# Reordering the first preparation of a gated mixture layer, and holding back two of its weight loads

## The chip, the cores and the metric

The kernel runs on one core of one Trainium2 chip. The metric is device time in microseconds (us) for one execution of the whole program, as the median of several runs. The profile is one further execution. Its view is given from the start of its span, and an engine is named as in the profile: PE is the tensor engine's matmul side, PEld its weight loads, DVE the vector engine, ACT the scalar engine, POOL GpSimd, SP the sync engine, whose work here is only to issue DMAs. ACTq and SPq are DMA issues by ACT and SP.

## The reference, cut to what matters

Four batches of 512 tokens with 512 channels pass one decoder layer in three stages, each closed by a residual and a LayerNorm:

```
x = layernorm(x + linear_attention(x))             # gated, 16 heads
x = layernorm(x + experts(x, fside, ctx))          # per batch an int8-style pair of linears
x = layernorm(x + gated_ffn(x))                    # top-2 of 8 LoRA experts

# experts, first linear (_smooth_quant_linear), per batch, w = fside[batch]:
amax_x = max|x| over tokens, amax_w = max|w| over rows     # the channel maxima
s  = sqrt(amax_x / amax_w); xs = x / s; ws = w * s         # then both are quantised by row

# gated_ffn:
logits = x @ gate_w.T;  top_w, top_i = top_k(logits, 2);  routing = softmax(top_w)
h1 = x @ w1.T + 2 * x @ A1.T @ B1.T    (h3 alike; A and B are the chosen expert's)
act = silu(h1) * h3;  out += routing * (act @ w2.T + 2 * act @ A2.T @ B2.T)
```

The precision is kept by splitting each fp32 operand into a high and a low part (`_hi`, `_lo`) and making three matmuls of each product (`matmul_split`, lines 116 to 118).

## The kernel before, in words

The program has two halves. The first half (up to 421 us in the profile) computes attention for all four batches with the quantised experts of batch 0 folded into it. The second half, the function `mixture`, runs over the four batches. For batch b it computes the gated layer of b and, threaded between its matmuls, the quantised experts of batch b+1. Every engine has its own program in it, and semaphores order them.

`mixture` has three kinds of section on each engine. `prepare(0)` runs once, ahead of everything. `hidden(b, ...)` runs over the 11 tiles f of the inner dimension: PE makes `f_h` (h1 in bank h1, h3 in bank h3) from the transposed tokens `f_xT` and the up-weights `f_up`, ACT takes silu, DVE weighs and multiplies. `between(b, ...)` makes the down matmuls and, beside them, the preparation for b+1. This case is about `prepare(0)`, for which there are no matmuls of another tile to run beside it.

What `prepare(0)` has to deliver:

- SP reloads x1 of batch 1 from DRAM into `tokens` (`load_expert_tokens`, line 1449) and fills the three slots of `f_up` with up tiles 0, 1 and 2 (`load_up`, line 1441). Then it goes on to `hidden`, where its first wait is for the end of tile 0.
- ACT issues the load of `fside[1]` into `weights` (`load_weights(0, 0)`, line 1617). That memory held the raw adapters before.
- PE makes the transposes of x, the logits by token (`logits_across`, `logits_by_token` L2250, in bank LT), and the adapters' inner products U1 and U3 in banks `f_z_sum` and `f_z_second`. Then it waits for DVE: `masks_transposed` (L2270) for the masks, `weights_spread` (L2280) for the routing weights, `first_maxima` (L2292) for the channel maxima and for `um_ready` at 4.
- DVE computes, from the logits, the choice of experts (`choose`, lines 1816 to 1840: 21 small instructions), the softmax weights (`weigh`, 1846 to 1850, with an exponential on ACT between), the masked adapters (`mask_adapters`, L1862, four products into `f_work`) and their low parts (`adapters_lo`, L1868). It also computes the channel maxima over token rows: `channel_top(b, 0, 0)` from `tokens` and `channel_top(b, 0, 1)` from `weights`, both L1931, both into `f_q_mem`. The second waits for the DMA of `weights`.
- ACT turns the masked adapters into high parts (`masked_hi`, L1589) and then writes `f_weightT` (`weights_out`, L1585). PE's first `f_h` matmul waits for the latter.

Engines take their instructions strictly in the order written. `first_maxima` reuses banks `f_z_sum` and `f_z_second`, and so comes after the masked adapters:

```
def first_maxima(b):
    for i, item in enumerate((MX0, MW0)):
        pe.wait_ge(top_ready, PRIMED + 4 * b + i + 1)
        if i == 0:
            pe.wait_ge(um_ready, PRIMED + 4 * b + 4)
```

Of the kernel before, what the change touches and what calls it, by code (L numbers as in the profile page):

```python
# [41 lines left out]
PRIMED = 1  # L42
# [1188 lines left out]
SLOTS = 3  # L1231
# [15 lines left out]
def mixture(nc, shared, used, x1_dram, x2_dram, up_dram, w1, w2, down_stream, descending, out_dram):  # L1247
# [9 lines left out]
    with ExitStack() as ctx:  # L1257
# [5 lines left out]
        def sem(name):  # L1263
            primed.append(ctx.enter_context(nc.semaphore("f_" + name)))
            return primed[-1]
# [108 lines left out]
        we_loaded = sem("we_loaded")  # L1374
# [26 lines left out]
        def slot(b, item):  # L1401

            k = BANK[item]
            return k, b * len(BANK_ORDER[k]) + BANK_ORDER[k].index(item)
# [5 lines left out]
        def place(b, key):  # L1410

            n = EXPERT_ORDER.index(key)
            return n % RING, b * EXPERT_PER_BANK + n // RING

        def batches(eng, prepare, hidden, between):


            prepare(0)
            with eng.Fori(0, B - 2) as b:
                hidden(b, True)  # L1420
                between(b, True, True)
            hidden(B - 2, True)
            between(B - 2, True, False)
            hidden(B - 1, False)
            between(B - 1, False, False)

        def tiles(b, f):
            return b * FT + f + 1
# [4 lines left out]
        @block.sync  # L1433
        def _(sp):
            sp.dma_start(desc[:, :], descending).then_inc(consts_loaded, 16)
            sp.dma_start(x2_dram[0:T, :].rearrange("(t p) d -> p t d", p=P), x2[:, :, :]).then_inc(x2_stored, 16)

            SLOT_USES = [len(range(r, FT, SLOTS)) for r in range(SLOTS)]

            def load_up(f):  # L1440
                sp.dma_start(up[:, f % SLOTS, :, :].bitcast(F32), up_dram[f, :, :, :])\
                    .then_inc(up_loaded[f % SLOTS], 16)

            def load_x3(source):
                sp.dma_start(x3[:, :, :], source.rearrange("(t p) d -> p t d", p=P)).then_inc(x3_loaded, 16)

            def load_expert_tokens(b):

                sp.dma_start(xe[:, :, :], x1_dram[bass.ts(b, T), :].rearrange("(t p) d -> p t d", p=P))\
                    .then_inc(xe_loaded, 16)  # L1450

            def tokens_transposed(b):
                for c in (KT - 1, KT - 2):
                    k, before = slot(b, XC0 + c)
                    sp.wait_ge(filled[k], PRIMED + before + 1)

            def store(b):
                for h in range(2):
                    sp.wait_ge(normed, PRIMED + b * TT + 2 * h + 2)
                    sp.dma_start(out_dram[bass.ds(b * T + h * 2 * P, 2 * P), :].rearrange("(t p) d -> p t d", p=P),  # L1460
                                 x3[:, 2 * h:2 * h + 2, :]).then_inc(out_stored, 16)

            def prepare(b):
                tokens_transposed(0)
                sp.wait_ge(x2_stored, PRIMED + 16)
                load_expert_tokens(0)
                for f in range(SLOTS):
                    load_up(f)

            def hidden(b, expert):  # L1470
                for f in range(FT - SLOTS):
                    sp.wait_ge(z_done, PRIMED + tiles(b, f))
                    load_up(f + SLOTS)
                    if f == 0:
                        sp.wait_ge(out_stored, PRIMED + 32 * b)
                        if expert:
                            load_x3(x1_dram[bass.ts(b, T), :])
                        else:
                            sp.wait_ge(x2_stored, PRIMED + 16 * (b + 1))
                            load_x3(x2_dram[bass.ts(b, T), :])  # L1480

            def between(b, expert, another):
                if expert:
                    sp.wait_ge(z_done, PRIMED + tiles(b, FT - 2))
                    load_up(0)
                    sp.wait_ge(summed, PRIMED + TT * (b + 1))
                    load_x3(x2_dram[bass.ts(b, T), :])
                    tokens_transposed(b + 1)
                    if another:
                        sp.wait_ge(x2_stored, PRIMED + 16 * (b + 2))  # L1490
                        load_expert_tokens(b + 1)
                    load_up(1)
                    load_up(2)
                store(b)

            batches(sp, prepare, hidden, between)
            sp.wait_ge(out_stored, PRIMED + 32 * B)

# [293 lines left out]
        def _(dve):  # L1792
# [12 lines left out]
            def x_lo(b, c):  # L1805
                k, n = slot(b, XC0 + c)
                dve.wait_ge(xT_hi_ready, PRIMED + b * KT + c + 1)
                dve.tensor_tensor(xT_lo[:, c, :], bank[k][:, :], xT_hi[:, c, :].bitcast(F32), ALU.subtract)\
                    .then_inc(drained[k], 1)
# [33 lines left out]
            def weigh(b):  # L1843

                dve.wait_ge(exp_ready, PRIMED + b + 1)
                dve.tensor_scalar(soft[:, 2, :], soft[:, 1, :], 1.0, None, ALU.add).then_inc(weight_ready, 1)
                dve.wait_ge(weight_ready, PRIMED + 3 * b + 1)
                dve.reciprocal(weight[:, 0, :], soft[:, 2, :]).then_inc(weight_ready, 1)
                dve.wait_ge(weight_ready, PRIMED + 3 * b + 2)
                dve.tensor_tensor(weight[:, 1, :], soft[:, 1, :], weight[:, 0, :], ALU.mult).then_inc(weight_ready, 1)  # L1850

            def mask_adapters(b):

                k, n = slot(b, MT)
                dve.wait_ge(drained[k], PRIMED + n + 1)
                for item in (U1, U3):
                    k, n = slot(b, item)
                    dve.wait_ge(filled[k], PRIMED + n + 1)
                for a in range(2):
                    for i, item in enumerate((U1, U3)):  # L1860
                        k, n = slot(b, item)
                        ins = dve.tensor_tensor(um[:, 2 * a + i, :], bank[k][:, :], maskT[:, a, :], ALU.mult)  # L1862
                        ins.then_inc(um_ready, 1)

            def adapters_lo(b):
                for a in range(4):
                    dve.wait_ge(um_hi_ready, PRIMED + 4 * b + a + 1)
                    dve.tensor_tensor(umT_lo[:, a, :], um[:, a, :], umT_hi[:, a, :].bitcast(F32), ALU.subtract)\  # L1868
                        .then_inc(um_lo_ready, 1)

            def prepare(b):
                x_lo(b, 0)
                x_lo(b, 1)
                dve.wait_ge(consts_ready, PRIMED + 3)
                dve.tensor_tensor(a_lo[:, :, :], a_raw, a_hi[:, :, :].bitcast(F32), ALU.subtract)\
                    .then_inc(consts_ready, 1)
                dve.tensor_tensor(b2_lo[:, :], b2_raw, b2_hi[:, :].bitcast(F32), ALU.subtract)\
                    .then_inc(consts_ready, 1)
                x_lo(b, 2)
                x_lo(b, 3)  # L1880
                for i in range(2):
                    channel_top(b, 0, i)
                dve.wait_ge(consts_loaded, PRIMED + 16)
                choose(b)
                weigh(b)
                mask_adapters(b)
                adapters_lo(b)
                channel_ratio(b, 0)
                channel_scale(b, 0)
# [29 lines left out]
            def channel_top(b, which, i):  # L1919

                C = CHANNELS[which]
                if i:
                    dve.wait_ge(we_loaded, PRIMED + 32 * b + 16 * which + 16)
                    if which:
                        k, n = place(b, (0, XT1))
                        dve.wait_ge(e_filled[k], PRIMED + n + 1)
                elif which == 0:
                    dve.wait_ge(xe_loaded, PRIMED + 16 * b + 16)
                else:
                    dve.wait_ge(e_act_ready, PRIMED + b + 1)  # L1930
                dve.tensor_reduce(top[:, i, 0:C], (xe, we)[i][:, :, 0:C].rearrange("p t c -> p c t"),  # L1931
                                  AX.X, ALU.max, apply_absolute_value=True).then_inc(top_ready, 1)
# [182 lines left out]
            def between(b, expert, another):  # L2115
# [14 lines left out]
                normalise(b, expert, another)  # L2130

            batches(dve, prepare, hidden, between)

        @block.tensor
# [406 lines left out]
```

## Time and profile before

| | us |
|---|---|
| median of 3 runs (lowest, highest) | 1150.32 (1149.33, 1150.97) |
| profiled execution, its own time | 1150.53 |
| its span | 1148.7 |
| PE busy | 1042.4 (91%) |
| DVE busy | 708.4 (62%) |
| ACT busy | 403.9 (35%) |
| POOL busy | 288.5 (25%) |

The profiled execution's time is 1.8 us more than its span (what lies around the first and the last instruction), and 0.2 us above the median. The granted clock of TensorE is 1.0 where it runs at 2.4 GHz and 0.50 at 1.2 GHz. Its mean over the span is 0.954. The busy shares are means over stages with different limits. What is asked here is what one stage of some 47 us costs, from 421 us, where the first half ends, to 468 us, where the first `f_h` matmul starts.

### The profile page before, as it was taken

Reading aid. Unit: us, or ns where it says so; the run is one execution under the profiler, and the core shown is the slowest. Engines: PE = TensorE matmul, PEld = TensorE weight load, DVE = VectorE, ACT = ScalarE, POOL = GpSimd, SP = SyncE. Lnnn points to the kernel's source line nnn. Section 1 sums busy time; section 2 is a strip of 40 time slices with the busy share of each in tenths; the row PEclk is TensorE's granted clock in tenths of the full one; section 3 lists DMA queues with packets and bytes.
Section 4 is the critical chain, followed back from the end, with each engine's and each line's share of the span. In section 5 each row is a group of like instructions: output and inputs, shape, how many; then the busy total and the mean of one; then the engine's idle time right before and its main releaser. Section 6 shows DMA issues by size and latency. Waiting matters only on the chain.

```text
span 1148.7 us, 14072 instructions
## 1 busy us (share of the span) xinstructions
PE 1042.4 (91%) x4920; PEld 820.0 (71%) x4920; DVE 708.4 (62%) x1150; ACT 403.9 (35%) x623; POOL 288.5 (25%) x239
## 2 busy tenths in 40 slices
PE   4899999999589635899999999999999999999997
PEld 3677777777477523777777777877777777878885
DVE  6544745746686744766764976773985864555542
ACT  4232423423134321453424253533343434322221
POOL 3245455554342110200142110131120132100021
PEclk9899999999899666899999999999999999999999
DMA  7013342532410016052446144337133417044421
GB/s 266 26 60 120 132 158 88 192 135 88 166 28 1 29 40 258 1 206 101 164 165 221 39 156 148 114 137 284 55 137 120 160 69 279 28 165 151 164 69 56
DMA packets 47852, 142.88 MB, mean 124 GB/s; under 512 B 3496, under 2 KB 14632, under 8 KB 42160
## 3 DMA queue, kind: packets, MB, share of 16 engines
q1 hardware_dynamic: 28720, 118.71, 28.2%
q10 hardware_dynamic: 19072, 23.35, 6.3%
q8 instruction: 39, 0.64, 0.2%
q14 instruction: 21, 0.17, 0.0%
HBM read 114.66 MB, written 27.39 MB: 124 GB/s over the span
## 4 chain that ended last, share of the span: by engine, by line
PE 41%; DVE 12%; DMA 3%; issue 3%; ACT 2%; POOL 1%; DVEq 0%; ACTq 0%
PE f_h L116 7%; PE f_h L118 7%; PE f_h L117 7%; PE f_h L2170 3%; PE f_y L116 3%; PE f_y L118 3%; PE f_y L117 3%; DMA f_down_raw<-in_down_stream 2%; DMA weights<-in_w 2%; DVE f_work L1911 2%; DVE f_work L1903 2%; PE f_y L2360 1%; DVE f_row_max L1981 1%; DVE f_q_mem L1931 1%; PE f_z_sum L116 1%
## 5 line engine op out<-in xcount | busy, mean ns | idle before, releaser
L116 PE MATMUL f_h<-f_xT_hi,f_up 128*128 128x512 f32 x352 | 139.8, 397 | 1.8 <-issue 1.1
L117 PE MATMUL f_h<-f_xT_hi,f_up 128*128 128x512 f32 x352 | 137.9, 392 | 0.0
L118 PE MATMUL f_h<-f_xT_lo,f_up 128*128 128x512 f32 x352 | 137.2, 390 | 0.0
L116 PE MATMUL ring<-w_hi,xT_hi 128*128 128x512 f32 x256 | 111.2, 434 | 15.1 <-DVE w_lo L754 15.1
L1503 POOL TENSOR_TENSOR f_down_lo<-f_down_raw,f_down_hi 128x512 fp32r<-128x512 f32 x44 | 61.0, 1389 | 229.6 <-ACT f_down_hi L1553 229.6
L1708 ACT ACTIVATE f_work<-f_h 128x512 f32<-128x512 f32 x88 | 52.4, 595 | 169.8 <-PE f_h L2170 114.5
L1903 DVE TENSOR_TENSOR f_work<-f_work,f_weightT 128x512 f32<-128x512 f32 x88 | 65.4, 743 | 70.0 <-ACT f_work L1708 69.0
L1514 POOL TENSOR_TENSOR weights<-weights,f_rows 128x512 f32<-128x512 f32 (+1 forms) x24 | 33.3, 1418 | 292.1 <-ACT f_rows L1635 182.5
L1911 DVE TENSOR_TENSOR f_work<-f_h,f_work 128x512 f32<-128x512 f32 x88 | 60.9, 692 | 70.1 <-PE f_h L118 64.8
L118 PE MATMUL ring<-w_lo,xT_hi 128*128 128x512 f32 x256 | 104.0, 406 | 0.0
L117 PE MATMUL ring<-w_hi,xT_lo 128*128 128x512 f32 x256 | 103.9, 406 | 0.0
L116 PEld LDWEIGHTS f_h<-f_xT_hi,f_up 128*128 128x128 f32 x352 | 66.1, 188 | 17.1 <-issue 2.3
L118 PEld LDWEIGHTS f_h<-f_xT_lo,f_up 128*128 128x128 f32 x352 | 66.1, 188 | 14.7
L117 PEld LDWEIGHTS f_h<-f_xT_hi,f_up 128*128 128x128 f32 x352 | 66.2, 188 | 14.0
L475 POOL TENSOR_TENSOR rot_b<-qk,ropes 128x256 f32<-128x256 f32 x64 | 55.5, 888 | 81.7 <-ACT qk L575 81.7
L116 PEld LDWEIGHTS ring<-w_hi,xT_hi 128*128 128x128 f32 x256 | 50.0, 195 | 32.0 <-issue 17.2
L116 PE MATMUL f_y<-f_down_hi,f_both_hi 128*128 128x512 f32 x176 | 72.5, 412 | 0.0
L117 PE MATMUL f_y<-f_down_hi,f_both_lo 128*128 128x512 f32 x176 | 71.1, 404 | 0.0
L118 PE MATMUL f_y<-f_down_lo,f_both_hi 128*128 128x512 f32 x176 | 70.8, 402 | 0.0
L2170 PE MATMUL f_h<-f_umT_hi,f_up 128*128 128x512 f32 x176 | 57.7, 409 | 11.4 <-DVE f_work L1911 11.4
L1602 ACT ACTIVATE f_second_hi<-f_work 128x512 fp32r<-128x512 f32 x44 | 27.9, 635 | 107.9 <-DVE f_work L1911 107.9
L575 ACT ACTIVATE qk<-ring 128x512 f32<-128x512 f32 x32 | 19.1, 597 | 121.0 <-PE ring L1063 121.0
(305 smaller groups left out, 2276.5 us busy)
## 6 DMA issues: line engine op xcount, KB each, us to landing
f_up<-up_scratch SPq DMA_DIRECT2D x44, 1408.0 KB, 6.1
f_down_raw<-in_down_stream ACTq DMA_DIRECT2D x44, 256.0 KB, 3.5
weights<-in_up_stream SPq DMA_DIRECT2D x11, 704.0 KB, 5.1
up_scratch<-tokens SPq DMA_DIRECT2D x11, 704.0 KB, 3.1
up_scratch<-scaled_w SPq DMA_DIRECT2D x11, 704.0 KB, 3.5
f_x<-x_scratch SPq DMA_DIRECT2D x7, 1024.0 KB, 8.6
x_tok<-in_x SPq DMA_DIRECT2D x4, 1024.0 KB, 5.5
out<-f_x SPq DMA_DIRECT2D x8, 512.0 KB, 3.0
```

The lines of the kernel that those rows point to most:

```text
L116: pe.matmul(out, lhs_hi, rhs_hi, start=start, stop=False)
L117: pe.matmul(out, lhs_lo, rhs_hi, start=False, stop=False)
L118: return pe.matmul(out, lhs_hi, rhs_lo, start=False, stop=stop)
L475: pool.tensor_tensor(b4[:, :, :, two], q4[:, :, :, 1 - two], sin[:, :, two].unsqueeze(1).to_broadcast([P, H, DK // 2]), ALU.mult).then_inc ...
L575: act.activation(qk[:, bass.ts((PQ, PK).index(item), D)], ring[k][:, :], ACT.Copy)\
L1503: pool.tensor_tensor(down_lo[:, f % DOWNS, :], down_raw[:, f % DOWNS, :], down_hi[:, f % DOWNS, :].bitcast(F32), ALU.subtract).then_inc(do ...
L1514: pool.tensor_tensor(we[:, t, 0:C], we[:, t, 0:C], rows[:, 1, 0:C], ALU.mult).then_inc(w_scaled, 1)
L1602: sc.activation(second_hi[:, :], act[:, 1, :], ACT.Copy).then_inc(act_hi_ready, 1)
L1708: sc.activation(silu[:, choice, :], h_ps[0][:, :], ACT.Silu).then_inc(silu_ready, 1)
L1903: dve.tensor_tensor(silu[:, choice, :], silu[:, choice, :], weightT[:, choice, :], ALU.mult)\
L1911: dve.tensor_tensor(act[:, choice, :], h_ps[1][:, :], silu[:, choice, :], ALU.mult)\
L2170: last = pe.matmul(h_ps[i][:, :], weights(f, l, cols), r[:, rhs, :], start=False, stop=True, skip_group_check=True)
```

## The change

Two edits, both in `prepare(0)` alone. On DVE, the choice of experts and their weights are put between the two channel maxima: the maxima of `tokens` stay in front, those of `weights` come behind `weigh` and ahead of `mask_adapters`. On SP, only up tile 0 is loaded at once. SP then waits until the DMA of `weights` has landed, and issues up tiles 1 and 2 after that. Instructions, shapes and data are the same, except for that one wait on SP.

```
@@ prepare(0) on SP
                 tokens_transposed(0)
                 sp.wait_ge(x2_stored, PRIMED + 16)
                 load_expert_tokens(0)
-                for f in range(SLOTS):
+                load_up(0)
+                sp.wait_ge(we_loaded, PRIMED + 16)
+                for f in range(1, SLOTS):
                     load_up(f)
@@ prepare(b) on DVE
                 x_lo(b, 2)
                 x_lo(b, 3)
-                for i in range(2):
-                    channel_top(b, 0, i)
+                channel_top(b, 0, 0)
                 dve.wait_ge(consts_loaded, PRIMED + 16)
                 choose(b)
                 weigh(b)
+                channel_top(b, 0, 1)
                 mask_adapters(b)
                 adapters_lo(b)
                 channel_ratio(b, 0)
```

## Rows read from the trace of the kernel before

**Rows 1.** Who waited for whom, 425 to 475 us: total, times, longest.

```profile
PE f_h L2270 <- DVE f_work L1840: 12.7, 1, 12.7
DVE f_q_mem L1931 <- DMA weights<-in_w: 10.3, 1, 10.3
```

**Rows 2.** Chain that ended last, 430 to 476 us: start us, us, what.

```profile
435.25 18.60 DMA weights<-in_w
...
461.64 1.05 PE f_h L2270 x8
...
463.77 0.70 DVE f_work L1862
464.49 2.42 ACT f_umT_hi L1589 x4
466.92 0.98 ACT f_weightT L1585 x2
...
468.14 0.49 PE f_h L116
468.63 0.23 PE f_h L117
```

**Rows 3.** DVE in order of time, 439 to 463 us: start us, us, instruction.

```profile
439.77 3.76 DVE L1931 TENSOR_REDUCE f_q_mem<-tokens 128x512 f32<-128x2048 f32 x1 [3.36 <-DMA tokens<-x_scratch]
453.87 3.62 DVE L1931 TENSOR_REDUCE f_q_mem<-weights 128x512 f32<-128x2048 f32 x1 [10.34 <-DMA weights<-in_w]
457.41 0.18 DVE L1816 COPY f_logits<-f_h 128x32 f32<-128x32 f32 x1
...
461.91 0.16 DVE L1850 TENSOR_TENSOR f_weight<-f_soft,f_weight 128x4 f32<-128x4 f32 x1
```

**Rows 4.** PE in order of time, 441 to 467 us: start us, us, instruction.

```profile
441.22 0.63 PE L118 MATMUL f_h<-f_xT_lo,f_a_hi 128*8 128x512 f32 x1
441.64 0.63 PE L116 MATMUL f_z_sum<-f_xT_hi,f_a_hi 128*128 128x512 f32 x1
...
444.90 1.05 PE L2250 MATMUL f_h<-ident,f_work 8*128 8x8 f32 x8
...
448.53 0.40 PE L118 MATMUL f_z_second<-f_xT_lo,f_a_hi 128*128 128x512 f32 x1
...
462.47 3.73 PE L2280 MATMUL f_h<-ident,f_weight 128*128 128x128 f32 x16
466.40 0.63 PE L2292 MATMUL f_z_sum<-ident,f_q_mem 128*128 128x128 f32 x4 [0.20 <-DVE f_work L1862]
```

**Rows 5.** DMA issues, 434 to 440 us: count, KB each, median us to landing.

```profile
f_up<-up_scratch SPq DMA_DIRECT2D x3, 1408.0 KB, 14.2
tokens<-x_scratch SPq DMA_DIRECT2D x1, 1024.0 KB, 5.7
```

**Rows 6.** DMA queues from 440 to 450 us (q1 is SP's, q10 ACT's): packets, MB, share.

```profile
q1 hardware_dynamic: 341, 3.48, 83.0%
q10 hardware_dynamic: 344, 0.70, 18.4%
```

**Rows 7.** Line 1617, the load of `weights`, over all six of its issues.

```profile
DMA to landing us min/median/max: 3.9/5.3/18.6
```

**Rows 8.** Line 2280 in the next batch, 596 to 792 us: busy us, mean ns.

```profile
L2280 PE MATMUL f_h<-ident,f_weight 128*128 128x128 f32 x16 | 1.9, 275 | 0.0
```

**Rows 9.** Windows: length, busy us (count) of PE, PEld, DVE, ACT, POOL, granted clock, DMA, GB/s.

```profile
343.60:347.00 3.40, 3.21 (x16) 2.93 (x17) 3.30 (x5) 3.38 (x6) 0.00 (x0) 0.52 0.00 0
...
412.50:415.30 2.80, 0.00 (x0) 0.00 (x0) 2.77 (x5) 0.00 (x0) 2.80 (x3) 0.97 0.00 0
...
436.50:442.60 6.10, 6.04 (x15) 2.51 (x16) 2.83 (x1) 0.70 (x2) 0.00 (x0) 0.51 1.04 424
...
448.90:452.80 3.90, 0.02 (x1) 0.00 (x0) 0.00 (x0) 0.00 (x0) 0.00 (x0) 0.99 0.67 273
...
461.60:466.50 4.90, 4.66 (x25) 4.40 (x26) 3.13 (x8) 3.03 (x5) 0.00 (x0) 0.52 0.00 2
```

More of the change, by code:

```diff
@@ L1466, in prepare @@
                 load_expert_tokens(0)
-                for f in range(SLOTS):
+                load_up(0)
+                sp.wait_ge(we_loaded, PRIMED + 16)
+                for f in range(1, SLOTS):
                     load_up(f)
@@ L1880, in prepare @@
                 x_lo(b, 3)
-                for i in range(2):
-                    channel_top(b, 0, i)
+                channel_top(b, 0, 0)
                 dve.wait_ge(consts_loaded, PRIMED + 16)
@@ L1885, in prepare @@
                 weigh(b)
+                channel_top(b, 0, 1)
                 mask_adapters(b)
```

## The prediction, made before the changed kernel had run

> **What bounds the kernel now.** I read four views in this order. The page says that PE is busy for 91% of the span, so a gain has to come from a place where PE stands idle. The waits around the start of `mixture` name such a place: PE stood 12.7 us in one piece ahead of L2270, the transposes of the masks, waiting for `choose`; and in the same stretch DVE stood 10.3 us ahead of L1931 for the DMA of `weights` [rows 1]. The chain says that both waits are one: it runs from the load of `weights`, issued at 435.25 and 18.60 us long, through DVE, to the masks on PE at 461.64, the masked adapters at 463.77, ACT's high parts and `f_weightT`, to the first `f_h` matmul at 468.14 [rows 2]. The timelines then show that the wait is due to order and not to need. The logits by token, all that `choose` reads, are complete when L2250 ends, at 444.90 + 1.05 = 445.95 [rows 4]. DVE has finished the maxima of `tokens` at 439.77 + 3.76 = 443.53 and then stands in front of a reduction of `weights` until 453.87; `choose` starts behind it at 457.41 [rows 3]. PE has had nothing to do since its last U3 matmul, 448.53 + 0.40 = 448.93 [rows 4].
>
> All that follows in the program hangs on that first `f_h` matmul: `hidden`, `between` and the later batches go from semaphore to semaphore, with no anchor in absolute time. A shift of its start should reach the end whole.
>
> **The change, part by part.**
>
> *When `choose` and `weigh` run.* They take from 457.41 to 461.91 + 0.16 = 462.07, so 4.66 us, ACT's exponential included [rows 3]. In the new order DVE is free at 443.53 and waits for the logits at 445.95. With a hand-off of about 0.05 us, `weigh` is complete at 445.95 + 0.05 + 4.66 = 450.66. ACT has nothing else to do there, so the exponential is as prompt as now.
>
> *The maxima of `weights`.* This reduction of 3.62 us [rows 3] now stands between `weigh` and `mask_adapters`. If the data are there by 450.66, it ends at 454.28, or 454.25 with the small overlap of successive DVE instructions that rows 3 show (453.87 + 3.62 is 457.49, the next starts at 457.41). Behind it on DVE are `mask_adapters`, `adapters_lo` and `channel_ratio`, and behind those all of `hidden`, so a late `weights` would still hold up everything.
>
> *When `weights` land.* Between 440 and 450 us both queues were full. SP's queue moved 3.48 MB in 341 packets and ACT's 0.70 MB in 344 [rows 6]. So `weights`, with small packets, got a sixth of the bandwidth while the three up tiles (1408 KB each [rows 5]) were under way. `tokens`, issued first, landed after 5.7 us, about 439.8, and this doesn't change [rows 5]. With one up tile in place of three, 1.44 MB at SP's rate of 0.348 MB/us is 4.1 us, so up tile 0 is done by about 443.5. `weights` then has 0.3 of its 1.05 MB. The other 0.75 MB at the summed rate of 0.42 MB/us is 1.8 us; with one or two us for the last packets, it lands between 445 and 447. The bounds: the fastest landing of this load is 3.9 us [rows 7], but not ahead of `tokens`, so about 440, and the slowest is as now, 453.85. Anything before 450.66 is worth the same. I take 446, as these are byte counts of the same transfers, which leaves 4 to 5 us of slack.
>
> *The held-back up tiles.* SP's wait ends at 446, and both tiles then take 2.88 MB at 0.42 MB/us, 7 us, with 2 us of latency: landed by about 455. Even if SP were released only at 453.9, it would be 463. PE wants up tile 1 only for f = 1, after the 30 matmuls and more of f = 0, some 10 us behind the first `f_h` matmul (in the old trace 478.7, so about 470 in the new). The edit costs nothing, and what hides it is tile 0. If the cover were gone the price would be the lateness itself. What is queued behind the waiting instruction on SP are these two loads, then a wait for the end of tile 0 that comes long after. Nobody else waits for SP.
>
> *From the masked adapters to PE.* The masks on PE start at about 450.3, and `f_maskT` is there two us later (1.05 and 1.03 us on PE and ACT now), before DVE is free at 454.25. So `mask_adapters` starts at 454.25 in place of 463.77 [rows 2]: 9.5 us earlier. From it to the first `f_h` matmul now takes 468.14 - 463.77 = 4.37 us over ACT's 2.42 and 0.98 us [rows 2], of which nothing changes: 458.6 in place of 468.1.
>
> *TensorE's clock.* This is the term that I can't read off. Now the clock fell some 3.9 us after PE stopped at 448.9, and in another place 2.8 us after PE stopped at 412.5 [rows 9]. PE then ran at half clock from 461.6 to 466.5, and the clock was back when the first `f_h` matmul came [rows 9]. In the new order PE stops for 1.4 us, transposes the masks, and spreads the weights in 1.9 us at full clock [rows 8] in place of 3.73 at half [rows 4], so until about 452.7. It then waits for all four masked adapters, 454.25 + 2.6 = 456.85 (they end so long after their start: 466.40 against 463.77 [rows 2, 4]). That is an idle gap of 4.1 us, as long as those behind which it fell. So I take it that the clock is at half when `first_maxima` starts. Eight transposes at half clock take about 2.0 us (16 took 3.73), ending at 458.85, so the first `f_h` matmul is at 458.85 and not 458.6: 0.25 us lost. After a restart the clock was back after 3.4 us in the quickest case, 4.9 us in the stage in question, and 6.1 us in the slowest of these [rows 9]. From 456.85 that is 460.3, 461.8 or 463.0, so `f_h` runs at half clock for 1.4 to 4.2 us. An `f_h` matmul starts 0.23 us after the one before it at full clock [rows 2] and one of that size 0.42 at half [rows 4], so 45% of that stretch is lost: 0.6 to 1.9 us. PE's first 30 matmuls of f = 0 are on the chain without a gap, so nothing hides this. I take 1.6 us, toward the long end, as the restart is interrupted by short gaps. Below nothing is not possible here, since the `f_h` matmuls already run at full clock.
>
> The Trainium skill, "TensorE: Matmul & The Clock Gate", section "Why this matters for your kernels", speaks against this change in part: it advises against idle stretches between matmul bursts, since the clock goes back to half behind them, and the new order leaves one right in front of the long run of `f_h`. By that rule the term is paid and the time is 1142.6; without it, 1140.8. The trace bears the rule out in both falls [rows 9], and no row shows a gap of that length that kept the clock.
>
> **The sum.** 9.5 - 0.25 - 1.6 = 7.7 us less. Against the profiled execution's 1150.53 that is 1142.8 (its span 1148.7 would become 1141.0). The median of the runs is 0.2 lower, so 1142.6.
>
> **The rivals.**
>
> *The clock doesn't fall, or the half-clock stretch is hidden.* The gain is the whole 9.5 us: 1140.8. For it: a little PE work, the masks and weights, now lies inside what was one long pause. Against: the gap of 4.1 us that stays behind it, and 2.8 us that were enough in rows 9.
>
> *`weights` still land late* (the two held-back tiles weren't what slowed it, so that half of the change does nothing). Then DVE stands again until 453.9, the masked adapters start at 457.5, 6.3 us earlier than now, and with the clock's 1.8 us the gain is 4.5: 1145.8. For it: only that the last packets of this load came 1.5 us or more after the queues thinned out. Against: rows 6, by which it got a sixth of the bandwidth, and rows 7, by which the same load lands in 3.9 to 5.3 us where it isn't crowded.
>
> *The gain is lost again later.* If something in `hidden` of batch 0 were bound by a transfer or an engine that doesn't shift, the time would be 1150. I find none: x3, up tile 3 and `scale_weights` on POOL are all issued from the ends of tiles and shift with them.
>
> *Slower.* The one mechanism that I see is the clock: if it stays at half through the first tiles of `hidden`, each us there costs 0.45. It decides from 9.5 / 0.45 = 21 us on, so until about 480; at 27 us it costs 12 and the time is 1153. No row with PE fully busy shows more than 6.2 us at half.
>
> **How the numbers follow.** Forecast (a gain of 5.8 to 8.6, as the clock term is 0.9 to 3.7): 0.72. Clock hidden, 1140.8: 0.13. `weights` late, 1145.8: 0.09. Gain lost later: 0.03. Slower: 0.03. The range from 1140.0 to 1145.4 takes in both bounds of the clock term, the case without it and the spread of single runs (1149.3 to 1151.0 before), and leaves out about 0.15 or 0.2. A difference of 0.2% (2.3 us) is about what a measurement of this kernel can tell from no change. Faster by more than that: 0.94; within it: 0.03; slower: 0.03.
>
> **What the new profile would show.** DVE's wait for `weights` gone, or under 0.5 us, with that load landing some 10 to 12 us after its issue in place of 18.6. L1816 right behind L2250, at about 446. L1931 on `weights` at about 450.7. L1862 at about 454.3. PE's wait ahead of L2270 down from 12.7 to 1.4 us, and a new one of about 4 us ahead of L2292 on L1862. The first `f_h` matmul at about 458.8, several of them at half clock, and the clock back between 460 and 463. No wait for up tile 1. From tile 1 on the same intervals as now, 7 to 8 us earlier. The prediction is wrong if `weights` land after 450.7, if the clock behaves otherwise, or if a later stage starts to wait for something new.

## The result and the profile after

The changed kernel takes 1141.76 us (median of 4 runs, 1140.74 to 1143.54) against 1150.53 before (4 runs, 1149.33 to 1150.97). The ratio is 0.9927, with a 95% interval of 0.991 to 0.9944, so it is 0.7% faster. The profiled execution has a span of 1140.4 us and a mean granted clock of 0.961, against 1148.7 and 0.954.

These are the waits of the changed kernel from 425 to 475 us (total, times, longest). Its lines lie two further down than before (L2270 is L2272 now).

```profile
PE f_z_sum L2294 <- DVE f_work L1864: 3.6, 1, 3.6
DVE f_q_mem L1933 <- DMA tokens<-x_scratch: 3.2, 1, 3.2
...
DVE f_logits L1818 <- PE f_h L2252: 2.6, 1, 2.6
...
PE f_h L2272 <- DVE f_work L1842: 1.4, 1, 1.4
```

Both waits of [rows 1] have turned into what was foreseen. DVE no longer waits for `weights` at all. PE waits 1.4 us for the masks in place of 12.7, and a new wait of 3.6 us stands ahead of `first_maxima`. The timeline of DVE shows the order and the times:

```profile
428.33 0.06 DVE L1795 MEMSET f_round_bias<- 128x1 f32 x1 [8.31 <-PEq L145]
...
438.70 3.77 DVE L1933 TENSOR_REDUCE f_q_mem<-tokens 128x512 f32<-128x2048 f32 x1 [3.24 <-DMA tokens<-x_scratch]
445.11 0.19 DVE L1818 COPY f_logits<-f_h 128x32 f32<-128x32 f32 x1 [2.64 <-PE f_h L2252]
...
449.70 3.65 DVE L1933 TENSOR_REDUCE f_q_mem<-weights 128x512 f32<-128x2048 f32 x1
453.27 0.68 DVE L1864 TENSOR_TENSOR f_work<-f_z_sum,f_maskT 128x512 f32<-128x512 f32 x1
```

The memset at 428.33 is DVE's first instruction in `mixture`. In the trace of before it stands at 429.29:

```profile
429.29 0.06 DVE L1793 MEMSET f_round_bias<- 128x1 f32 x1 [8.32 <-PEq L145]
```

So `mixture` starts 0.96 us earlier in this execution, after a first half that the change doesn't touch. It is chance: in the other traces of this document the memset stands anywhere from 426.67 to 429.79, and in the changed kernel's second one at 429.73. All comparisons of stages below are therefore made from that memset. The masked adapters start 24.94 us behind it (453.27 - 428.33) and not 34.48 us (463.77 in [rows 2], less 429.29): 9.54 us less. PE and its clock:

```profile
449.84 2.41 PE L2282 MATMUL f_h<-ident,f_weight 128*128 128x128 f32 x16
455.89 1.08 PE L2294 MATMUL f_z_sum<-ident,f_q_mem 128*128 128x128 f32 x4 [3.64 <-DVE f_work L1864]
456.76 1.06 PE L2294 MATMUL f_z_second<-ident,f_q_mem 128*128 128x128 f32 x4
457.63 0.79 PE L116 MATMUL f_h<-f_xT_hi,f_up 128*128 128x512 f32 x1
458.22 0.63 PE L117 MATMUL f_h<-f_xT_hi,f_up 128*128 128x512 f32 x1
458.64 0.63 PE L118 MATMUL f_h<-f_xT_lo,f_up 128*128 128x512 f32 x1
...
466.65 0.63 PE L2172 MATMUL f_h<-f_umT_hi,f_up 128*128 128x512 f32 x2
```

The same stretch in windows (length, busy us of PE, PEld, DVE, ACT and POOL with counts, granted clock, DMA share, GB/s):

```profile
452.30:455.40 3.10, 0.00 (x0) 0.00 (x0) 3.10 (x5) 1.42 (x3) 0.00 (x0) 0.96 0.65 272
455.50:462.10 6.60, 6.21 (x19) 5.10 (x20) 4.79 (x12) 3.36 (x6) 0.00 (x0) 0.51 0.00 0
462.30:466.60 4.30, 4.30 (x20) 3.54 (x19) 0.69 (x1) 1.88 (x2) 0.00 (x0) 1.00 0.00 0
```

The clock fell at about 455.2, 2.9 us after PE had stopped at 452.25, and came back at about 462.0, so 4.4 us of `f_h` ran at half. The reader sees it in the matmuls as well: they start 0.43 us apart at 458.22 and 458.64, where [rows 2] have 0.23. The 30 matmuls of f = 0 ahead of L2172 take 466.65 - 457.63 = 9.02 us. In the trace of before they took 475.12 - 468.14 = 6.98:

```profile
475.12 0.63 PE L2170 MATMUL f_h<-f_umT_hi,f_up 128*128 128x512 f32 x2
```

So the half clock cost 2.04 us. The transfers of the changed kernel between 434 and 475 us (count, KB each, median us to landing):

```profile
f_up<-up_scratch SPq DMA_DIRECT2D x3, 1408.0 KB, 9.3
weights<-in_w ACTq DMA_DIRECT2D x1, 1024.0 KB, 11.7
```

`weights` was issued at 434.29 and landed at 446.0, 11.7 us after its issue in place of 18.6.

### The profile page after: what moved, and what is told of

The parts are those of the page before. It is cut to its first block, busy times and chain, and to the rows that moved or that the text cites. A ratio compares the mean times of both kernels' runs of the same rounds, so it can differ in the third digit from the quotient of the medians.

```text
span 1140.4 us, 14072 instructions
## 1 busy us (share of the span) xinstructions
PE 1038.0 (91%) x4920; PEld 816.6 (72%) x4920; DVE 708.3 (62%) x1150; ACT 404.0 (35%) x623; POOL 289.1 (25%) x239
## 4 chain that ended last, share of the span: by engine, by line
PE 41%; DVE 14%; issue 3%; ACT 2%; DMA 2%; DVEq 0%; ACTq 0%
PE f_h L116 7%; PE f_h L117 7%; PE f_h L118 7%; PE f_h L2172 4%; PE f_y L116 2%; PE f_y L118 2%; PE f_y L117 2%; DMA f_down_raw<-in_down_stream 2%; DVE f_work L1913 2%; DVE f_q_mem L1933 2%; DVE f_work L1905 2%; PE f_y L2362 1%; PE f_z_sum L116 1%; PE f_z_sum L117 1%; DVE f_row_max L1983 1%
## 5 line engine op out<-in xcount | busy, mean ns | idle before, releaser
L116 PE MATMUL f_h<-f_xT_hi,f_up 128*128 128x512 f32 x352 | 140.8, 400 | 0.6 <-issue 0.6
L116 PE MATMUL ring<-w_hi,xT_hi 128*128 128x512 f32 x256 | 111.1, 434 | 15.1 <-DVE w_lo L754 15.1
L116 PEld LDWEIGHTS f_h<-f_xT_hi,f_up 128*128 128x128 f32 x352 | 66.6, 189 | 16.0 <-issue 1.1
L116 PEld LDWEIGHTS ring<-w_hi,xT_hi 128*128 128x128 f32 x256 | 50.0, 195 | 32.0 <-issue 17.2
L116 PE MATMUL f_y<-f_down_hi,f_both_hi 128*128 128x512 f32 x176 | 70.6, 401 | 0.0
L2172 PE MATMUL f_h<-f_umT_hi,f_up 128*128 128x512 f32 x176 | 57.7, 409 | 12.2 <-DVE f_work L1913 12.2
```

The source lines that it names most:

```text
L116: pe.matmul(out, lhs_hi, rhs_hi, start=start, stop=False)
L2172: last = pe.matmul(h_ps[i][:, :], weights(f, l, cols), r[:, rhs, :], start=False, stop=True, skip_group_check=True)
```

## The experiments

Two measures are given for each run. One is the median over 4 to 6 runs, which moves by about one us between groups of runs (the changed kernel gave 1141.76 and, a second time, 1142.76; the kernel before gave 1150.53, 1149.98 and 1150.34). The ratio is taken to the runs of the kernel before that stood beside each group. The other, from the profile, is the stage: from the memset that opens `mixture` on DVE to the first L2172 (L2170), the end of the first 30 `f_h` matmuls. It is split where `f_h` starts. Each of its parts repeats within 0.05 us in the two profiles of the changed kernel, so it separates what the medians can't.

| kernel | to first `f_h` | 30 `f_h` matmuls | stage | median | ratio to before, 95% |
|---|---|---|---|---|---|
| before | 38.85 | 6.98 | 45.83 | 1150.53 | |
| changed | 29.30 | 9.02 | 38.32 | 1141.76 | 0.9927 (0.991 to 0.9944) |
| changed, again | 29.33 | 9.02 | 38.35 | 1142.76 | 0.9935 (0.9916 to 0.9954) |
| loads held, old order | 32.00 | 6.98 | 38.98 | 1144.98 | 0.9961 (0.9945 to 0.9976) |
| new order, loads not held | 32.46 | 7.57 | 40.03 | 1146.74 | 0.9964 (0.995 to 0.9978) |
| changed, clock kept | 29.35 | 7.00 | 36.35 | 1140.54 | 0.9918 (0.9904 to 0.9931) |
| only tile 2 held | 29.27 | 8.99 | 38.26 | 1143.13 | 0.9941 (0.9924 to 0.9957) |
| all three held | 29.32 | 9.02 | 38.34 | 1142.44 | 0.9933 (0.9913 to 0.9954) |
| all held, split maxima | 27.51 | 9.80 | 37.31 | 1142.15 | 0.9929 (0.9913 to 0.9945) |
| the same, clock kept | 27.58 | 6.99 | 34.57 | 1138.65 | 0.9895 (0.9878 to 0.9913) |

**Each half of the change alone.** The edit on SP without the one on DVE:

```
-                for f in range(SLOTS):
+                load_up(0)
+                sp.wait_ge(we_loaded, PRIMED + 16)
+                for f in range(1, SLOTS):
                     load_up(f)
```

> The kernel before with the edit on SP alone: up tiles 1 and 2 wait for weights, DVE keeps its old order. My theory, from the traces of before and after: weights land about 446, as in the changed kernel, so DVE stands some 3.5 us for them in place of 10.3, choose runs behind the second maxima from about 449.6 and the masked adapters start at about 455.9 (7 us earlier than before, 2.6 us later than in the changed kernel). PE's restart from the masks to the first f_h matmul is then one nearly unbroken run, as before the change, so the clock should be back to 2.4 GHz when f_h starts and nothing is paid for it: 7 us faster than before, 1143.6, and only some 1 to 2 us slower than the changed kernel although its masked adapters are 2.6 us later. First rival, that the order of DVE's work is what helped and the loads don't matter: no change, 1150.5. Second rival, that the clock costs the same here: 1145.5.

And the edit on DVE without the one on SP:

```
-                for i in range(2):
-                    channel_top(b, 0, i)
+                channel_top(b, 0, 0)
                 dve.wait_ge(consts_loaded, PRIMED + 16)
                 choose(b)
                 weigh(b)
+                channel_top(b, 0, 1)
                 mask_adapters(b)
```

> The changed kernel with all three up tiles loaded at once again: the edit on DVE alone. My theory: weights land 18.6 us after their issue, at about 452.9, the second maxima end at 456.5 and the masked adapters start there, 6.3 us earlier than before; PE stands from about 452 to 459, so the first f_h matmuls run at half clock and some 1.9 us is lost: 4.4 us faster than before, 1146.1. First rival, that the two loads didn't slow weights: the same as the changed kernel, 1141.8. Second rival, no cost of the clock: 1144.2.

With the loads held and the old order, DVE and PE did this:

```profile
446.11 3.73 DVE L1933 TENSOR_REDUCE f_q_mem<-weights 128x512 f32<-128x2048 f32 x1 [3.70 <-DMA weights<-in_w]
...
456.13 0.69 DVE L1864 TENSOR_TENSOR f_work<-f_z_sum,f_maskT 128x512 f32<-128x512 f32 x1 [1.70 <-ACT f_maskT L1580]
...
460.55 0.49 PE L116 MATMUL f_h<-f_xT_hi,f_up 128*128 128x512 f32 x1 [0.72 <-ACT f_weightT L1587]
```

and in windows

```profile
452.00:458.70 6.70, 4.56 (x24) 4.26 (x24) 4.76 (x16) 3.08 (x6) 0.00 (x0) 0.50 0.37 156
458.90:467.50 8.60, 7.88 (x38) 6.42 (x38) 4.96 (x12) 4.72 (x7) 0.00 (x0) 1.00 0.00 0
```

The masked adapters start 27.6 us after the memset (at 428.55 here), 6.9 us less than before, and the clock is back at about 458.7, before `f_h` begins; PE had been at work since 454.0. The stage is 6.85 us shorter, as the theory had it, and the rival that only the order matters falls. The median is only 5.0 us below that of the kernel before in the runs beside it (1149.98), 1144.98 where 1143.6 was expected. In its profile 0.7 us of the stage's gain are lost after the stage, and that profile is of the fastest of the six executions (1143.57). The rest is not explained.

With the new order and the loads not held, DVE waited for `weights` again, and PE longer than in any other run with the new order:

```profile
454.21 3.62 DVE L1931 TENSOR_REDUCE f_q_mem<-weights 128x512 f32<-128x2048 f32 x1 [3.07 <-DMA weights<-in_w]
457.75 0.68 DVE L1862 TENSOR_TENSOR f_work<-f_z_sum,f_maskT 128x512 f32<-128x512 f32 x1
...
460.37 1.09 PE L2292 MATMUL f_z_sum<-ident,f_q_mem 128*128 128x128 f32 x4 [6.77 <-DVE f_work L1862]
```

and, in the window from PE's restart until the clock was back,

```profile
460.40:463.40 3.00, 3.00 (x11) 2.61 (x12) 2.97 (x6) 2.74 (x4) 0.00 (x0) 0.51 0.00 0
```

`weights` took 18.6 us to land, exactly as before the change, so the two up tiles are what slowed it. The masked adapters start 6.4 us earlier than before (28.10 against 34.48), as expected (6.3). The clock was back 3.0 us after PE's restart at 460.37, when 1.25 us of `f_h` had passed, so it cost 0.6 us and not 1.9, and the stage is 5.8 us shorter where 4.4 was expected. The median of 1146.74 lies near the expected 1146.1 all the same, which is chance: in this profile 1.5 us of the stage's gain are lost again after the stage.

What follows: each half does most of the work alone, 6.85 and 5.8 us in the stage, and both together give 7.5 and not 12.7. They remove the same wait from two sides. What holding the loads adds to the new order is 3.2 us in the start of `f_h`, and what the order adds to the held loads is 2.7, of which the clock takes back 2.0.

**The clock.** The changed kernel with work for PE in its pause:

```
                 weights_spread(b)
+                for _ in range(14):
+                    pe.matmul(y_ps[0][:, :], a_hi[:, 0, 0:P], xT_hi[:, 0, :], start=True, stop=True)
                 first_maxima(b)
```

> The changed kernel with 14 further matmuls of 512 columns on PE between weights_spread and first_maxima, into a bank that nothing reads before it is overwritten. They fill the 3.6 us in which PE waits for the masked adapters. My theory: f_h starts at the same time, 457.6, but at full clock, so the 2.0 us that the half clock cost come back: 1139.7. Rival, that the half-clock stretch is hidden or that these matmuls run long and delay first_maxima: no change, 1141.8, or slower by what they overrun (14 x 0.23 = 3.2 us from 452.2 end at 455.5, before 455.9, so under 0.2 us at full clock, but 2.5 us if they ran at half clock).

```profile
452.40:456.10 3.70, 3.19 (x14) 2.30 (x14) 3.70 (x6) 1.89 (x4) 0.00 (x0) 1.00 0.59 249
456.10:464.80 8.70, 8.01 (x38) 6.58 (x39) 5.12 (x12) 4.87 (x7) 0.00 (x0) 1.00 0.00 0
```

The clock stayed at 2.4 GHz throughout. `f_h` starts at the same distance as in the changed kernel (29.35 and 29.30), and its 30 matmuls take 7.00 us in place of 9.02. So the half clock is the whole of those 2.0 us, and the rival, that they are hidden, falls. The median is 1140.54, 0.8 us above the expected 1139.7, and 1.2 to 2.2 us below the two medians of the changed kernel. The intervals of the ratios overlap, so it is the stage that shows the gain.

**How much slack the load of `weights` has.** With two up tiles at once in place of one:

```
                 load_up(0)
+                load_up(1)
                 sp.wait_ge(we_loaded, PRIMED + 16)
-                for f in range(1, SLOTS):
-                    load_up(f)
+                load_up(2)
```

> The changed kernel with up tiles 0 and 1 loaded at once and only tile 2 held back behind weights. By the byte counts (two tiles of 1.44 MB at 0.348 MB/us from about 438.3, then the rest of weights at 0.42 MB/us and one or two us for the last packets) weights land between 449 and 450.2, where DVE wants them at 449.7. My theory: a wait of DVE for weights of 0.5 us at the most, so the same time as the changed kernel, 1141.8, to 0.5 us more. Rival, that DVE reads weights while other loads slow it, or that tile 2 comes late for its use: a longer reduction than 3.65 us or a wait of PE for up tile 2, 1143 or more.

With none at once:

```
-                load_up(0)
                 sp.wait_ge(we_loaded, PRIMED + 16)
-                for f in range(1, SLOTS):
+                for f in range(SLOTS):
                     load_up(f)
```

> The changed kernel with all three up tiles held back behind weights and nothing else. My theory: weights land near 443, 3 us earlier than in the changed kernel, which nobody needs, since DVE gets to them at 449.7: the same stage time as the changed kernel, within 0.2 us, and 1141.8. Rival, that the changed kernel was still limited by the landing of weights: up to 2 us faster; or that up tile 0 is late: slower, with a wait of PE for f_up.

`weights` with two tiles beside it, and then with none:

```profile
weights<-in_w ACTq DMA_DIRECT2D x1, 1024.0 KB, 15.3
```

```profile
weights<-in_w ACTq DMA_DIRECT2D x1, 1024.0 KB, 7.5
```

So the landing takes 7.5, 11.7, 15.3 and 18.6 us with none, one, two and three tiles beside it (6.8 and 6.9 with none in the two runs with split maxima below): 3.3 to 4.2 us for each. At the rates of [rows 6], 1.44 MB take 3.4 us of both queues together and 4.1 of SP's alone. The stage is the same with none, one and two (38.34, 38.32, 38.26), and DVE has no wait for `weights` in any of them. With two it landed just in time, some 15.3 us after an issue about 6 us behind the memset, where DVE gets to it 21.3 us behind it. The expected wait of up to 0.5 us didn't appear, and neither did a late tile. To hold back one tile was enough for the profiled stage, by a margin too small to rely on. Its median of 1143.13 is 0.8 us above what was expected at the most, and the profile is of the fastest of the four executions (1140.47), so it can't be said that all of them were free of the wait. With all three held the median is 1142.44, and nothing is gained or lost in the stage, as expected.

**The order taken further.** All three tiles held, and the maxima of `weights` in two halves, the first in DVE's pause ahead of `choose`:

```
                 channel_top(b, 0, 0)
+                dve.wait_ge(we_loaded, PRIMED + 16)
+                weights_top(0)
                 dve.wait_ge(consts_loaded, PRIMED + 16)
                 choose(b)
                 weigh(b)
-                channel_top(b, 0, 1)
+                weights_top(1).then_inc(top_ready, 1)
                 mask_adapters(b)
...
+            def weights_top(half):
+                cols = bass.ts(half, D // 2)
+                return dve.tensor_reduce(top[:, 1, cols], we[:, :, cols].rearrange("p t c -> p c t"),
+                                         AX.X, ALU.max, apply_absolute_value=True)
```

> The changed kernel with all three up tiles held back behind weights, and the maxima of weights cut into two reductions of 256 columns each: the first in DVE's pause ahead of choose, the second where the whole stood, behind weigh. My theory: with no up tile beside it, weights land near 443, the first half runs to about 445 or 446, choose starts with or within 1 us of the logits (445.1), the second half ends near 452 and the masked adapters start there, 1.2 to 1.8 us earlier than in the changed kernel. PE's pause ahead of first_maxima shrinks from 3.6 to about 2 us. If the clock then stays up, the stage is 3.3 to 3.8 us shorter than in the changed kernel (1138.2); if it falls as it did, 1.2 to 1.8 us (1140.3). Rival, that up tile 0 comes too late for the first f_h matmul (issued at 443, it lands at about 449 by the same byte counts, 7 us ahead): a wait of PE for the DMA of f_up, and no gain, 1141.8.

```profile
448.80:453.00 4.20, 2.29 (x19) 1.91 (x16) 4.20 (x6) 2.84 (x5) 0.00 (x0) 1.00 0.75 318
453.10:454.30 1.20, 1.06 (x8) 0.82 (x8) 1.20 (x3) 1.20 (x3) 0.00 (x0) 0.91 0.00 0
454.50:461.10 6.60, 6.27 (x15) 4.95 (x16) 3.00 (x9) 1.57 (x3) 0.00 (x0) 0.52 0.00 0
```

`f_h` starts 1.8 us earlier than in the changed kernel (27.51 against 29.30), as expected, but its 30 matmuls take 9.80 us: the clock fell although the pause was only 1.9 us long, and stayed low for the first 6.1 us of `f_h`. Of the 1.8 us, 0.8 are lost so, and the median shows no difference from the changed kernel. Of the two forecasts the one with a falling clock was nearer, and even that was 0.2 to 0.8 us too good in the stage and 1.9 in the median. Up tile 0 was in time, so that rival falls. With PE kept busy in the pause as well:

```
                 weights_spread(b)
+                for _ in range(7):
+                    pe.matmul(y_ps[0][:, :], a_hi[:, 0, 0:P], xT_hi[:, 0, :], start=True, stop=True)
                 first_maxima(b)
```

> The kernel with the split maxima and all three up tiles held back, and with 7 further matmuls of 512 columns on PE between weights_spread and first_maxima, as in the run that kept the clock. My theory: both gains add, as the one is when the masked adapters start and the other is at what clock the first f_h matmuls run: f_h starts at about 456 at full clock, 10.9 to 11.3 us less in the stage than before, 1138.2. Rival, that the split alone keeps the clock: then this one is no faster than that, and slower by what the 7 matmuls overrun.

```profile
457.40:464.30 6.90, 6.90 (x30) 5.69 (x31) 3.29 (x9) 3.07 (x4) 0.00 (x0) 1.00 0.00 0
```

Both gains are there, 27.58 and 6.99 us, and the stage is 11.26 us shorter than before. The median of 1138.65 makes it the fastest of all; its interval (0.9878 to 0.9913) touches that of the changed kernel (0.991 to 0.9944) only at the edge.

The changed kernel once more, beside these:

> The changed kernel as it is, beside the others on the same chip. My theory: from the first instruction of mixture to the last h matmul of tile 0, 38.3 us in place of 45.8, of which the place where the clock rises can move 1 to 2 us from run to run; median 1141.8. Rival, none: this is the measure of the spread.

Its stage was 38.35 us, the same as the first time; the 1 to 2 us by which the rise of the clock was thought to move didn't appear. The profiled execution took 1145.41 us all the same, 3.2 more than the first one's 1142.24. Of these, 1.4 lie ahead of the memset and 1.8 behind the stage.

## Why the prediction was right

It forecast 1142.6, and the median is 1141.76 (1142.76 the second time). By its own steps:

- *When `choose` and `weigh` run.* Right. The logits' copy starts 0.11 us after L2252 ends (445.11 against 443.95 + 1.05 = 445.00), and the maxima of `weights` begin at 449.70, 4.6 us later.
- *The maxima of `weights`.* 3.65 us, in line with 3.62. That it lies on the path is shown by the split: 1.8 us of it taken off the path brought `f_h` forward by 1.8.
- *When `weights` land.* In the time of the old trace it landed at 446.0 + 0.96 = 447.0, at the late end of the 445 to 447 that I gave, and 1 us later than the 446 that I took. The working itself says 446.3 to 447.3 (443.5, 1.8, and one or two us). The slack was 3.7 us and not 4 to 5. The runs with none, two and three tiles beside it confirm the count of bytes.
- *The masked adapters.* 9.54 us earlier, 9.5 forecast.
- *The held-back tiles* cost nothing. The waits show none for `f_up`.
- *From the masked adapters to the first `f_h` matmul.* 4.36 us, with 4.37 before. The 0.25 us that I added for `first_maxima` at half clock isn't there. The `f_h` matmul waits for ACT's `f_weightT` too, and starts 0.26 us behind the end of it in both traces (457.63 and 457.37 after, 468.14 and 467.88 before); PE's slower transposes lie beside ACT's work. In all ten traces, at either clock, this stretch is 4.36 to 4.42 us. ACT before and after:

```profile
466.82 1.06 ACT L1585 ACTIVATE f_weightT<-f_h 128x512 f32<-128x512 f32 x2
```

```profile
456.31 1.06 ACT L1587 ACTIVATE f_weightT<-f_h 128x512 f32<-128x512 f32 x2
```

- *The clock.* That it falls, that it costs and that nothing hides the cost was right, and is shown by the run that kept the clock. The size was 2.04 us, where I had put 1.6 (1.85 with the 0.25) and 1.9 at the most: the clock was back 6.1 us after the restart, the slowest case of [rows 9], and 4.4 us of `f_h` ran at half. The 3.7 us that the chances use as the upper bound of this term follow from no row. The pause was 3.64 us and not 4.1, as the spread of the weights took 2.41 us at full clock and not the 1.9 of [rows 8]. The rule that the prediction weighed, from the Trainium skill, "TensorE: Matmul & The Clock Gate", section "Why this matters for your kernels", against idle stretches between bursts, holds here: the trace of the changed kernel agrees (the clock fell 2.9 us into a pause of 3.6), and to fill the stretch is worth what it cost.
- *The sum.* 7.7 us forecast, 7.51 us in the stage. The span fell by 8.3, which is these 7.5 and the 0.96 by which `mixture` began earlier, less 0.2 further on. That it came so close is luck in part: the 0.25 too much and the 0.44 too little work against each other, and the other kernels of this document paid anything from nothing to 2.8 us for the clock, which the old trace could not foretell.

That the stage's gain reaches the end whole was only argued. From the memset to the end of the span the program took 719.4 us before and 712.1 after, so in this pair of traces it is true but for 0.2 us. It isn't true of every trace: behind the stage the program takes 673.6 us before, 673.8 after and 673.7 to 673.8 in three of the experiments, but 675.5 in the changed kernel's second trace, 674.3 with the loads held alone and 675.1 with the order alone. In the second trace the cause is the clock. In the old trace it fell for a while near the end of `hidden` in batches 0 to 2, and in the first trace of the changed kernel it didn't. The same stretch, 585 to 600 us, in the old trace and in the new:

```profile
585.00:600.00 15.00, 12.60 (x48) 9.78 (x47) 10.43 (x21) 4.57 (x8) 4.86 (x4) 0.89 0.43 155
```

```profile
585.00:600.00 15.00, 12.71 (x60) 10.06 (x58) 6.01 (x11) 9.10 (x15) 4.25 (x4) 1.00 0.77 277
```

One would expect a further gain from the three dips that are gone. There is none, since PE waits there for ACT's normalised tokens: 13.19 us from the last L2170 of that `hidden` (L2172) to the transposes of the next batch in both traces, with 0.73 us of waiting in the old and 2.29 in the new.

```profile
591.76 0.40 PE L2170 MATMUL f_h<-f_umT_lo,f_up 128*128 128x512 f32 x1
604.95 1.06 PE L2231 MATMUL f_h<-ident,tokens 128*128 128x128 f32 x8 [0.73 <-ACT tokens L1677]
```

```profile
583.28 0.39 PE L2172 MATMUL f_h<-f_umT_lo,f_up 128*128 128x512 f32 x1
596.47 1.07 PE L2233 MATMUL f_h<-ident,tokens 128*128 128x128 f32 x8 [2.29 <-ACT tokens L1679]
```

The change didn't do away with the dips. The second trace of the same kernel has them again behind batches 1 and 2, and so has every trace of the experiments behind at least one batch. Where such a dip comes late it does cost time. This is the stretch around the transposes behind batch 2, in the first and in the second trace of the changed kernel:

```profile
950.57:960.57 10.00, 8.51 (x44) 5.75 (x45) 3.86 (x5) 5.17 (x9) 2.59 (x2) 1.00 0.76 249
```

```profile
952.00:962.00 10.00, 8.11 (x36) 6.29 (x37) 3.84 (x5) 5.30 (x10) 2.65 (x3) 0.83 0.62 189
```

In the second, the down matmuls behind the transposes start 0.43 us apart and not 0.23 until 958.3, and the first adapter matmul of the next batch (L116, `f_h<-f_xT_hi,f_a_hi`) comes 7.97 us behind the transposes (961.59 - 953.62) and not 6.46 (958.41 - 951.95). That is 1.5 of the 1.8 us which this execution lost behind the stage.

So the spread of the single executions lies outside the stage: the memset that opens `mixture` moves by 3.1 us between the ten traces, what lies behind the stage by 1.9, and the stage of the changed kernel by 0.03. What decides in which executions the clock falls there stays open, and so do the 1.4 us by which the median with the loads held alone lies above its own profile.

## What to carry to other kernels

Where an engine with a strict order stands in front of a late transfer, look for work behind it whose operands are long complete. Both ways out, to move that work ahead and to give the transfer the bandwidth, remove the same wait, so their gains don't add. A pause that is made shorter or moved changes the clock of what follows: fill the pause (this worked in both runs that did it), and count the half-clock matmuls before believing a gain of a few us. A measure of the stage from one of its own instructions to another separates what whole-program medians can't.

## What the runs showed of the hardware that was not expected

- A shorter pause didn't cost less. With 3.6 us between PE's bursts the half clock cost 2.0 us, with 1.9 us it cost 2.8 and with 6.8 us it cost 0.6. In the second case the granted clock fell about 1.0 us after PE was back at work (within window 453.10 to 454.30 above). The stretches at half were about equally long, 6.8 us each: 455.2 to 462.0, 454.1 to 460.9 and 456.5 to 463.4. What differs is how much of `f_h` they covered: 4.4, 6.1 and 1.25 us. Where the fall and the rise lie against the work decides the cost, more than the length of the pause.
- Two queues shared the DMA engines packet by packet: 341 and 344 packets in 10 us, for 3.48 and 0.70 MB [rows 6]. Each further up tile of 1.44 MB put off the landing of `weights`, 1 MB in small packets, by 3.3 to 4.2 us, though with one tile ahead of it `weights` had been issued only 0.8 us later.
- A small DVE instruction took long once: L1984 on 128x4 took 1.32 us in the run with all tiles held, where the same instruction takes 0.17 us in the nine other traces. PE then waited 1.4 us for DVE ahead of the next L2171, where the changed kernel shows 0.17. POOL was at work on `weights` at that moment, but it was in the changed kernel too (from 472.03 for 7.3 us, with the instruction at 476.26 and 0.17 us long), so POOL alone doesn't explain it. The cause is open.

```profile
475.42 1.32 DVE L1984 TENSOR_SCALAR f_scale<-f_row_max 128x4 f32<-128x4 f32 x1
```
